# A two-layer recurrent block on one core: another order at the end of the scan, a shift in three transfers, and a split prologue

## The reference, cut to what matters

```
q = xn @ W_up.T;  v = xn @ W_v.T
d = 1
while d < 512:                       # 9 levels: 1, 2, 4, ... 256
    left = concat([identity] * d, q[:, :-d])
    val = (left + q) @ W             # W: orthogonal factor of W_scan_raw
    att = softmax(per-token scores of 4 lanes of left against 4 lanes of q)
    z = att @ val, per token;  q = left + rms_norm(z) / (1, 2, 3, 4)
    d *= 2
s = (q * v) @ W_proj.T
f = sum over 8 experts e of gate[:, e] * (relu(xn @ w1[e] + b1[e]) @ w2[e] + b2[e])
```

## Time and profile before

| what | value |
|---|---|
| median of 3 runs | 585.0 us (581.9 to 585.72) |
| profiled execution, time | 585.52 us |
| profiled execution, span from first to last instruction | 583.8 us |
| busy: PE, DVE, POOL, ACT | 523.2, 478.0, 378.7, 292.1 us |
| mean granted TensorE clock | 0.96 of full |

### The profile page before, as it was taken

One profiled execution on the slowest core, in us unless ns is written; L12 is line 12 of the kernel. 1 busy time (PEld: TensorE's weight loads), 2 busy tenths in 40 slices (PEclk: granted clock), 3 DMA queues, 4 the chain that ended last, 5 costly groups with the idle time before them and its releaser, 6 DMA issues.

```text
span 583.8 us, 8819 instructions
## 1 busy us (share of the span) xinstructions
PE 523.2 (90%) x2918; PEld 406.9 (70%) x2918; DVE 478.0 (82%) x882; ACT 292.1 (50%) x792; POOL 378.7 (65%) x326
## 2 busy tenths in 40 slices
PE   3978999999999999578799999999999999999854
PEld 3745666666666666366678888878878888887733
DVE  7677786877776567996988999999999999999945
ACT  3432342243235234444566776676676677667423
POOL 6930010021203445685799999999999999999951
PEclk9989999999999999868799999999999999999859
DMA  7530000000000000001011011101101110110002
GB/s 231 170 145 0 2 1 1 1 1 11 9 0 4 16 1 1 15 18 41 18 56 32 26 54 37 55 19 55 38 20 54 37 42 33 37 37 20 20 0 72
DMA packets 16601, 20.81 MB, mean 36 GB/s; under 512 B 2344, under 2 KB 10160, under 8 KB 16428
## 3 DMA queue, kind: packets, MB, share of 16 engines
q1 hardware_dynamic: 16556, 20.26, 11.4%
HBM read 9.76 MB, written 1.05 MB: 19 GB/s over the span
## 4 chain that ended last, share of the span: by engine, by line
PE 61%; ACT 18%; DVE 12%; issue 5%; DMA 3%; POOLq 0%; POOL 0%; ACTq 0%; SPq 0%; DVEq 0%
PE bank L563 59%; ACT shared L1116 6%; ACT bank L1125 4%; ACT shared L1086 3%; DMA left_tok<-state_ext 2%; ACT z_ln L1108 2%; PE bank L566 2%; DVE bank L1521 2%; DVE shared L1546 1%; DVE shared L1515 1%; DVE shared L1265 1%; DVE z_ms L1535 1%; DVE ln_stats L1198 1%; DMA x<-in_x 0%; DVE shared L1348 0%
## 5 line engine op out<-in xcount | busy, mean ns | idle before, releaser
L563 PE MATMUL bank<-xnT_lo,wgu_hi 128*128 128x512 f32 x264 | 121.1, 459 | 6.1 <-DVE h_shared L1233 3.6
L563 PE MATMUL bank<-w,shared 128*128 128x128 f32 x1024 | 124.2, 280 | 0.3
L563 PEld LDWEIGHTS bank<-w,shared 128*128 128x128 f32 x1024 | 118.3, 194 | 6.1 <-ACT shared L1116 6.0
L563 PE MATMUL bank<-xnT_hi,wgu_lo 128*128 128x512 f32 x264 | 106.1, 402 | 0.0
L563 PE MATMUL bank<-xnT_hi,wgu_hi 128*128 128x512 f32 x264 | 105.3, 399 | 0.0
L501 POOL TENSOR_TENSOR shared<-shared 128x1024 f32<-128x1024 f32 x36 | 86.1, 2393 | 15.2 <-DVE shared L1546 15.2
L563 PE MATMUL bank<-shared 128*128 128x512 f32 (+3 forms) x280 | 89.2, 442 | 1.2 <-ACT shared L966 1.2
L988 ACT ACTIVATE shared<-bank 128x512 f32<-128x512 f32 x68 | 40.7, 598 | 97.0 <-PE bank L563 92.3
L1546 DVE TENSOR_TENSOR shared<-shared,bank 128x2048 f32<-128x2048 f32 x36 | 82.0, 2278 | 1.8 <-PE bank L563 1.8
L1521 DVE TENSOR_REDUCE bank<-shared 128x64 f32<-128x2048 f32 x36 | 82.4, 2289 | 0.2
L1116 ACT ACTIVATE shared<-bank,b 128x512 f32<-128x512 f32 x128 | 82.0, 700 | 0.2
(11 more groups left out here) (176 smaller groups left out, 799.2 us busy)
## 6 DMA issues: line engine op xcount, KB each, us to landing
w<-in_w SPq DMA_DIRECT2D x8, 256.0 KB, 2.7
shared<-in_w SPq DMA_DIRECT2D x1, 2048.0 KB, 9.4
left_tok<-state_ext SPq DMA_DIRECT2D x16, 128.0 KB
left_tok<-state_ext SPq DMA_DIRECT2D x8, 192.0 KB
shared<-in_wd SPq DMA_DIRECT2D x1, 1088.0 KB, 12.1
x<-in_x SPq DMA_DIRECT2D x4, 256.0 KB, 3.6
out<-x SPq DMA_DIRECT2D x4, 256.0 KB, 2.3
left_tok<-state_ext SPq DMA_DIRECT2D x4, 254.0 KB
```

The source lines that it names most:

```text
L563: return nc.tensor.matmul(out, lhsT, rhs, start=start, stop=stop)
```

## The change

Three parts.

- **Prologue.** Batch 0's logits go ahead of the turning of batch 1, into another bank, and get an exponential of their own; DVE does `route_groups(0)` and `route_tops(0)` ahead of the folding of `attn_w`. The two splits of twelve units become six of four units.
- **Shift.** For d = 1 the transfer of partitions 1 to 127 becomes one of 1 to 112 and one of 113 to 127.
- **End.** The gates of batch b are turned at the end of PE's slots 29 to 32 (`turn_gates`) and copied by ACT; PE multiplies them by `b2` in slots 30 to 33, behind `values`, all in bank 0; DVE adds them (`bias_sum`) in the same slots, behind `products`. Second values are computed in slots 33 and 34. ACT takes the silus behind slot 34. Step 35's mix is summed on DVE, not on POOL, and DVE's last instructions get an order of their own.

The diff, cut to its core:

```diff
-            sp.wait_ge(s("w_lo_done"), 6)
+            sp.wait_ge(s("w_lo_done"), 10)
...
+                if d == 1:
+                    sp.dma_start(left_tok[d:P - 15, b], state_ext[0:P - 16, b, 1:TB + 1]).then_inc(s(f"ld_left{b}"), 16)
+                    sp.dma_start(left_tok[P - 15:P, b], state_ext[P - 16:P - 1, b, 1:TB + 1]).then_inc(s(f"ld_left{b}"), 16)
+                elif d < P:
+                    sp.dma_start(left_tok[d:P, b], state_ext[0:P - d, b, 1:TB + 1]).then_inc(s(f"ld_left{b}"), 16)
                 if d < P:
-                    sp.dma_start(left_tok[d:P, b], state_ext[0:P - d, b, 1:TB + 1]).then_inc(s(f"ld_left{b}"), 16)
                     sp.dma_start(left_tok[0:d, b], state_ext[P - d:P, b, 0:TB]).then_inc(s(f"ld_left{b}"), 16)
...
-            split_weights(0, wg, slice(5, UNITS), 4)
-            split_weights(1, wu, slice(5, UNITS), 5)
+            for n in range(3):
+                split_weights(0, wg, slice(5 + 4 * n, 9 + 4 * n), 4 + 2 * n)
+                split_weights(1, wu, slice(5 + 4 * n, 9 + 4 * n), 5 + 2 * n)
...
             tokens_to_channels0(0)
-            tokens_to_channels0(1)
             pe.wait_ge(s("ld_gate0"), 16 * 2)
             router_logits0(0)
+            tokens_to_channels0(1)
...
+            def turn_gates(k, b):                       # PE, end of slots 29 to 32
+                pe.wait_ge(s("sumT_cp"), k + 2)
+                pe.wait_ge(s("gate1_done"), 2)
+                for j in range(TB):
+                    last = tr(bank[0][0:E1, j * P:(j + 1) * P], gate1[:, b * TB + j])
+                last.then_inc(s("g1T_mm"), 1)
+            def gated_biases(b):                        # PE, slots 30 to 33, behind values
+                pe.wait_ge(s("g1T_cp"), b + 1)
+                for j in range(TB):
+                    last = mm(bank[0][:, j * P:(j + 1) * P], gate1T[:, j * P:(j + 1) * P], b2[:])
+                last.then_inc(s("acc_mm"), 1)
+            def second_values(b):
+                if b == 0:
+                    pe.wait_ge(s("ffn_relu"), E1 * B * HC)
+                elif b == B - 1:
+                    pe.wait_ge(s("v1_cp"), V1.index(V1[b]) + 1)
+                mm(bank[V1[b]][:], l1_w[:, 1], xnT[:, b * N:(b + 1) * N]).then_inc(s("v1_mm"), 1)
...
+            def gates_out(b):                           # ACT, end of slots 29 to 32
+                act.wait_ge(s("g1T_mm"), b + 1)
+                after(act, s("acc_mm"), b)
+                a.copy(gate1T, bank[0][0:E1, :]).then_inc(s("g1T_cp"), 1)
...
+            k = LEVELS * B - 1                          # ACT, behind slot 34
+            slot(k - 1, B - 2, v1=(B - 1,))
             for b in range(B):
-                act.wait_ge(s("acc_done"), b + 1)
+                act.wait_ge(s("ffn_acc"), (E1 - 2) * B + b + 1)
                 a.activation(acc[...], acc[...], ACT.Silu).then_inc(s("gl1_done"), 1)
+            a.preload_act_table_set(EXP_LN)
+            square(k - 1, B - 2); expo(k, B - 1); rsqrt(k - 1, B - 2); square(k, B - 1); rsqrt(k, B - 1)
...
+            def bias_sum(blk):                          # DVE
+                dve.wait_ge(s("acc_mm"), blk + 1)
+                dve.wait_ge(s("ffn_acc"), (E1 - 3) * B + blk + 1)
+                tt(part, part, bank[0][:], ALU.add).then_inc(s("acc_done"), 1)
             def slot(k, b, this=True, before=True, summed=None):
                 if this:
                     products(k, b)
+                if 0 <= k - (E1 - 1) * B - 2 < B:
+                    bias_sum(k - (E1 - 1) * B - 2)
                 if summed:
                     expert_sum(*summed)
...
+            slot(LEVELS * B - 2, B - 2, summed=(E1 - 1, B - 1))
+            k, b = LEVELS * B - 1, B - 1
+            products(k, b); gate_state(0); scores(k, b); score_max(k, b); softmax_shift(k, b)
+            square_sum(k - 1, b - 1); exp_sum(k, b); mix_values(k, b)
+            tt(mix2, mix[..0:2], mix[..2:4], ALU.add)   # was POOL's halve_mix, 1024 elements
+            tt(zb, m[:, :, 0], m[:, :, 1], ALU.add)     # was POOL's add_lanes, 512 elements
+            gate_state(1); output(0); square_sum(k, b); output(1); gate_state(2)
+            tt(zb, zb, z_r, ALU.mult); tt(x_tok[:, b], z[:, b % 2], left_tok[:, b], ALU.add)
+            output(2); gate_state(3); output(3)
```

More of the change, by code:

```diff
@@ L555, in _ @@
             slot(top * B + 3, 3, ahead=False)
-            slot(top * B + 4, 0, this=False, ahead=False)
-            slot(top * B + 5, 1, this=False, before=False, ahead=False)
+            scale_z(top * B + 2, 2)
+            new_state(top * B + 2, 2)
         @block.tensor
@@ L874, in expert_down, with slot @@
                     last.then_inc(s("ffn_down"), 1)
-            def slot(k, b, this=True, ahead=True, up=None, down=None, then=None):
-                if this:
-                    values(k, b)
+            def slot(k, b, up=None, down=None, v1=(), turn=None):
+                values(k, b)
+                if down and down[0] == E1 - 1:
+                    gated_biases(down[1])
                 if down:
                     expert_down(*down, range(TB))
-                if then:
-                    then()
                 if up:
@@ L891, in slot @@
                     expert_up(*up, 3)
+                for n in v1[2:]:
+                    second_values(n)
+                if turn is not None:
+                    turn_gates(k, turn)
             down(B * PAIRS - 2)
@@ L910, in _ @@
                 n = k - 2
-                slot(k, k % B, up=divmod(n + 1, B) if n + 1 < E1 * B else None, down=divmod(n, B))
-            slot(LEVELS * B - 2, B - 2, then=gated_biases)
-            slot(LEVELS * B - 1, B - 1, ahead=False)
-            pe.wait_ge(s("ffn_acc"), (E1 - 1) * B)
-            pe.wait_ge(s("acc_done"), B)
-            for b in range(B):
-                mm(bank[FREE[b]][:], l1_w[:, 1], xnT[:, b * N:(b + 1) * N]).then_inc(s("v1_mm"), 1)
-            pe.wait_ge(s("mix_done"), LEVELS * B)
-            pe.wait_ge(s("prod_done"), LEVELS * B)
-            def final_state(b):
-                pe.wait_ge(s("xtok_done"), LEVELS * B + b + 1)
+                turn = n + 1 - (E1 - 1) * B
+                slot(k, k % B, up=divmod(n + 1, B) if n + 1 < E1 * B else None, down=divmod(n, B),
+                     v1=(0, 1, 2) if n + 1 == E1 * B else (), turn=turn if 0 <= turn < B else None)
+            slot(LEVELS * B - 2, B - 2, v1=(B - 1,))
+            values(LEVELS * B - 1, B - 1)
+            def final_state(b):
+                if b < B - 1:
+                    pe.wait_ge(s("xtok_done"), LEVELS * B + b + 1)
+                else:
+                    pe.wait_ge(s("last_state"), 1)
+                read, count = (("sumT_cp", LEVELS * B), ("prod_done", LEVELS * B), ("mix_done", LEVELS * B), ("v1_cp", 1))[b]
+                pe.wait_ge(s(read), count)
                 for j in range(TB):
@@ L1125, in gated, with slot @@
                     a.activation(acc[:, t] if e == 0 else y, y, ACT.Copy, scale=gate1[:, t, e:e + 1]).then_inc(s("ffn_gated"), 1)
-            def slot(k, b, this=True, before=True, ahead=True, up=None, down=None, then=None):
-                if ahead:
-                    left_out(k + 1, (b + 1) % B)
-                if this:
-                    expo(k, b)
-                if before:
-                    square(k - 1, (b - 1) % B)
-                if then:
-                    then()
+            def slot(k, b, up=None, down=None, v1=(), turn=None):
+                left_out(k + 1, (b + 1) % B)
+                expo(k, b)
+                square(k - 1, (b - 1) % B)
                 if down:
@@ L1140, in slot @@
                     relu(*up, 1)
-                if before:
-                    rsqrt(k - 1, (b - 1) % B)
-                if ahead:
-                    sum_in(k + 1, (b + 1) % B)
+                rsqrt(k - 1, (b - 1) % B)
+                sum_in(k + 1, (b + 1) % B)
                 if up:
@@ L1147, in slot @@
                     relu(*up, 3)
+                for n in v1:
+                    second_values_out(n)
+                if turn is not None:
+                    gates_out(turn)
             act.wait_ge(s("silu_done"), item(B * PAIRS))
@@ L1611, in gate_state @@
                 tt(qvT[:, b], v1T[:, b], bank[b][:], ALU.mult).then_inc(s("qv_done"), 1)
-            gate_state(0)
-            gate_state(1)
-            slot(LEVELS * B, 0, this=False)
             def output(b):
```

129 lines of the change are left out of this document (75 added, 54 removed).

## The result

The changed kernel takes 592.6 us (median of 4 runs, 591.2 to 593.7) against 585.4 us for the kernel before (4 runs): ratio 1.013 (95% interval 1.008 to 1.018). It is slower by 1.3%, above the range of 576 to 591. Its profiled execution has a span of 590.8 us (before 583.8), so 7.0 us are to be found, where the forecast's sum was -1.2.

What follows compares the result with a forecast made beforehand. It took PE and ACT as the bound, with DVE almost a second bound in the steady slots. Prologue -4.3, shift -4.3 and end +7.4 sum to -1.2 us on 585.52, so 584 us; range 576 to 591.

Steps and rivals of the forecast that it cites:

- The prologue: Start of the kernel: earlier routing and shorter POOL holds bring PE's gate rows earlier, -4.3 us, ends -6 and -1.
- The rival of 1 us: Prologue: DVE is held until POOL is through, so it gives only 1 us; 587 us, chance 0.1.
- The shift: Start of the scan: POOL's and ACT's waits for batch 3's shift go, -4.3 us, ends -3.5 and -6.5.
- The rival of nothing: Shift at the scan's start: no faster in two parts, so the waits stay; 588 us, chance 0.07.
- what is late next is DVE's own maximum and shift: Start of the scan: DVE's maximum and shift, ready at 265.77, limit the gain to 4.3 us, not 6.1.
- the far end: Shift's end of -6.5 us: the loss of clock from 287 to 296 us, 0.73 over 9 us, goes too.
- Slots 30 to 33: DVE's bias_sum waits for PE's biases with the softmax behind it: 5.3 + 3 x 2.6 = +13.1 us.
- 3 x 2.6: Slots 30 to 33: a period of 11.2 us against 8.57, +2.6 us a slot, for three slots.
- The first term: First of slots 30 to 33: expert_sum starts 7.0 us behind products, formerly 1.7; +5.3 us.
- The rival of a falling clock: Slots 30 to 33: PE idles and its clock falls, +10 us over four slots; 594, or 589 with two; chance 0.15.
- my threshold of 0.8: Slots 30 to 33: the falling PE clock decides once a slot's granted clock is under 0.8.
- Behind the slots: From products(35) to the end of the span: 27 us instead of 32.7, -5.7 us, ends -3.5 and -8.

Runs made afterwards that it cites:

- experiment 1: Kernel before with only the changed prologue and the shift in three transfers, old end in every engine; 575.65 us, ratio 0.984.
- experiment 2: Changed kernel with one swap on VectorE: expert_sum ahead of bias_sum in slots 30 to 33; 587.2 us, ratio 1.003.
- experiment 4: Changed kernel with one edit at the end of PE's order: project(2) ahead of final_state(3); 591.3 us, ratio 1.0105.
- experiment 3: Changed kernel with bias_sum moved behind mix_values on VectorE, the last expert's sum waiting for it; 580.6 us, ratio 0.992.
- 8, both: Changed kernel with bias_sum behind mix_values on VectorE and project(2) ahead of final_state(3) on PE; 577.0 us, ratio 0.987.
- 9, biases behind down: Changed kernel with bias_sum behind mix_values, project(2) ahead of final_state(3), and PE's gated_biases behind expert_down; 577.3 us, ratio 0.987.
- 10, and the gates' copy later: Changed kernel with late bias_sum, project(2) ahead of final_state(3), gated_biases behind expert_down, and ACT's gates_out behind the next slot's square; 577.1 us, ratio 0.987.

## Why the prediction was wrong

| kernel (us) | a slot, 30 to 33 | T29 to P35 | P35 to end | median |
| --- | --- | --- | --- | --- |
| before, and 1 | 8.57 | 47.4, 47.3 | 32.7 | 585.4, 575.65 |
| after | 13.2 | 66.6 | 30.8 | 592.6 |
| 2, expert sum first | 10.87 | 59.0 | 30.9 | 587.2 |
| 4, projection first | 13.2 | 66.7 | 27.8 | 591.3 |
| 3, late bias sum | 10.09 | 53.3 | 29.6 | 580.6 |
| 8, both | 10.09 | 53.3 | 28.4 | 577.0 |
| 9, biases behind down | 9.63 | 53.2 | 28.8 | 577.3 |
| 10, and the gates' copy later | 9.64 | 53.2 | 27.8 | 577.1 |

- **The prologue** (-4.3) held: -4.6 by the medians, -3.2 between traces with the same clock. The -4.6 between the two profiled traces is near the forecast in part by luck, since 1.4 of it is the low clock of that one execution of before. Both of its halves were needed, which the prediction argued only in one direction. The rival of 1 us is out: a step of 12 elements took 0.17 us in the changed kernel, and 3.38 before. A step that starts beside a piece of GpSimd's ends when the piece ends, but VectorE does get steps in between two pieces.
- **The shift** (-4.3) held: -3.8 by the trace of the shift alone, -4.9 by the medians. The rival of nothing is out. The step "what is late next is DVE's own maximum and shift" is what the trace shows, 0.32 us between it and the sum. Behind it, 2 us more went with PE's clock in the changed kernel, as the far end had allowed: `values(4)` to `values(5)` took 8.56 us for 10.88. Experiment 3 with the same shift has 10.99 there, so this part isn't the change's to promise.
- **Slots 30 to 33** (+13.1) is the step that failed, in its term 3 x 2.6: the period of 11.2. The first term held: from `products(30)` to `products(31)` it is 13.88 us for 8.57, +5.3 as forecast (in experiment 2, without the missed wait, 13.29). The next three take 13.2 us each, +4.65 and not +2.6, and 3 x 2.05 are the 6.1 us missing. The mechanism held as far as it went: VectorE does wait for PE's biases, and without the missed wait (experiment 2) the slot is 10.87, T29 to P35 +11.6. What I left out is the other direction. Putting `bias_sum` ahead of `expert_sum` delays `expert_sum` too, and PE's next `down` waits for that one (it writes the bank that the sum reads). I had asked who is queued behind the waiting instruction on VectorE and named the softmax and ACT's exponential, but not the semaphore that the next instruction in the queue signals. The round then closes through `down` and ScalarE's `gated`, in 13.2 us and with slow matmuls, and not through VectorE's softmax. It made +19.2 out of the +13.1.
- **The rival of a falling clock** was given 0.15 and 589 to 594, and the measured time lies in it; but its account was only half right. It put the idling of PE down to VectorE's lag and the price on the matmuls in VectorE's wait; `values` and the biases take 1.06 and 1.15 us there, no longer than in experiment 2. In the trace the long matmuls are those of `down`, behind a wait that I had not seen, and the clock of a slot was 0.87, above my threshold of 0.8. By my own rule for it the rival should not have decided, yet 1.60 of the 2.35 us a slot are longer matmuls. So the rule was wrong too, and not only the slot.
- **Behind the slots** (-5.7) came as -1.8. Three things were off. The first is PE's order: I summed VectorE's instructions and took PE's projections as ready; standing behind `final_state(3)` costs `project(2)` 2.1 us (experiment 4). The second is PE's clock: the last projection takes 2.08 us, 0.9 above that of experiment 4, and I had left this open (1.2 to 2.1). The third is VectorE's sum of 1024 elements, 1.98 us and not 1.2 (+0.8): GpSimd's last addition runs beside it until 571.66. 27 + 2.1 + 0.9 + 0.8 = 30.8. `gate_state(0)`'s wait (2.69) and the silus with their two table loads, in time, were as said.
- **The signs.** I had written that I am wrong if the slots stay under 9.5 us, the clock in them is under 0.8, or the gate rows come before 40 or after 44. None of these came: 13.2 us, 0.87, 40.22. A slot longer than forecast was not among the signs; VectorE's wait of 4.2 us where about 2 was said is the one that told.
- **The range** left the case of two engines holding each other out. Its upper end, +15 for the whole end, was made of known terms at their far ends; the end measured +17.4.

The best of these is experiment 1, 575.65 us: the new end costs 5.9 us up to P35 even in its best order, and gives back 4 to 5 behind it. That its additions lie where PE and VectorE have no room is argued from their rows (PE busy for 36.65 of 38.50 us in experiment 3). The old end did the same work where both engines waited anyway (5.47 us of PE). Whether a third place for the biases would do better wasn't tried.

## What to carry to other kernels

When an instruction that waits goes into an engine's queue, follow every instruction behind it to its own semaphore, and ask of each waiter whether the first wait depends on it in turn: here two engines that waited for each other once a round cost 2.35 us a round, the longer matmuls behind the wait included. If the added work has slack, put it where its operand is long there; here one addition moved behind the mix was worth 12 us. And where a chain at the end is dominated by one engine, write down the order of the engine that feeds it too: a ready product behind an unready one cost 2.1 us.

## What the runs showed of the hardware

VectorE's small steps ended with GpSimd's instruction, for casts as for subtractions. GpSimd's pieces in the changed kernel:

```profile
22.01 0.60 POOL L389 CAST wgu_hi<-shared 128x512 fp32r<-128x512 f32 x1
22.69 1.30 POOL L391 TENSOR_TENSOR wgu_lo<-shared,wgu_hi 128x512 fp32r<-128x512 f32 x1
23.94 0.63 POOL L389 CAST wgu_hi<-shared 128x512 fp32r<-128x512 f32 x1
```

and VectorE beside them:

```profile
22.06 0.59 DVE L1285 TENSOR_TENSOR shared<-shared 128x16 f32<-128x16 f32 x1
22.69 0.17 DVE L1292 TENSOR_TENSOR shared<-shared 128x12 f32<-128x12 f32 x1
22.78 1.24 DVE L1290 TENSOR_TENSOR shared<-shared 128x4 f32<-128x4 f32 x1
23.94 0.15 DVE L1292 TENSOR_TENSOR shared<-shared 128x8 f32<-128x8 f32 x1
24.02 0.57 DVE L1290 TENSOR_TENSOR shared<-shared 128x8 f32<-128x8 f32 x1
```

The cast from 22.01 holds a step of 16 elements for 0.59 us, the subtraction from 22.69 one of 4 for 1.24, the cast from 23.94 one for 0.57; at each of these boundaries a step of 0.15 to 0.17 us gets through. The Trainium skill, SBUF — State Buffer (Who interferes with whom), says that a VectorE instruction with two SBUF inputs contends with a GpSimd instruction that reads SBUF, and that whichever starts first holds the pair for its whole length. The trace agrees, for GpSimd's casts too; the page's own words on copies and casts are of VectorE's. What didn't follow is that VectorE is shut out until GpSimd is through. The operations with an operand in a bank (`shared_hidden`, 0.67 at 27.83) and MATCH_REPLACE8 (0.17) ran beside these pieces at their usual length.

A transfer of 112 partitions and one of 15 took the place of one of 127 and removed a wait of 6.2 us. The Trainium skill, DMA: Bandwidth & Descriptors (Rules for kernel authors), speaks against two transfers to disjoint partition halves, since both use all sixteen engines; here the one of 127 had used one of sixteen (DMA share 0.06), and the rule's reason doesn't apply.

Of PE's clock: in the kernels with the new shift, `values(0)` to `values(5)` took from 50.8 to 53.6 us with the same work in it (57.1 to 57.4 with the old shift). The granted clock from 245 to 262 us was 0.53 in the changed kernel and 0.73 in experiment 3, and yet the changed kernel took less for the whole, 52.1 us for 53.2. A difference of 2 us between two single traces in such a stretch isn't yet one between two kernels.
